# Multi-query attention of a fused decoder: score and probability banks apart, the value product in halves, the bias on GpSimd

## What is computed

```python
qkv = einsum('bsd,ed->bse', layernorm(x), Wqkv_w) + Wqkv_b
q = qkv[..., :256].reshape(B, S, 16, 16).transpose(0, 2, 1, 3)
k = qkv[..., 256:272]
v = qkv[..., 272:]
scores = einsum('bhqd,bkd->bhqk', q, k) * 16 ** -0.5
scores = where(causal, scores, finfo.min)
attn = softmax(scores, axis=-1)
ctx = einsum('bhqk,bkd->bqhd', attn, v).reshape(B, S, 256)
x = x + einsum('bsd,ed->bse', ctx, out_w) + out_b
```

## Time and profile before

| | |
|---|---|
| median of 3 runs | 3217.69 us (3211.05 to 3225.68) |
| the profiled execution | 3207.37 us, span 3205.5 us |
| PE busy over the span | 2644.7 us (83%) |
| DVE busy | 2030.2 us (63%) |
| ACT busy | 1581.7 us (49%) |
| POOL busy | 1372.7 us (43%) |

### The profile page before, as it was taken

The page is one execution under the profiler, slowest core; times in us unless marked ns, Lnnn a source line. Parts: engine busy times, 40 slices in busy tenths (PEclk is TensorE's granted clock), DMA queues, the critical chain, the costliest instruction groups (busy, mean ns, idle before and its releaser), DMA issues. The chain is left out here.

```text
span 3205.5 us, 85997 instructions
## 1 busy us (share of the span) xinstructions
PE 2644.7 (83%) x33006; PEld 1936.5 (60%) x33006; DVE 2030.2 (63%) x3706; ACT 1581.7 (49%) x2950; POOL 1372.7 (43%) x1490
## 2 busy tenths in 40 slices
PE   3888888888858888867677779999999999997565
PEld 2677777777732222224466667888788888886333
DVE  6888888888858888848577743434343434334776
ACT  3555555555527777731334313443434444443566
POOL 4888888888822333224222212222222212221665
PEclk9999999999969999979799989999999999999667
DMA  3000000000013333300100020000000000000000
GB/s 120 2 0 0 0 0 0 0 0 0 0 49 89 89 90 90 92 13 0 31 24 25 26 69 6 7 6 7 6 7 6 7 6 7 5 33 1 13 16 23
DMA packets 94784, 77.50 MB, mean 24 GB/s; under 512 B 17520, under 2 KB 88560, under 8 KB 93424
## 3 DMA queue, kind: packets, MB, share of 16 engines
q1 hardware_dynamic: 94576, 74.35, 7.6%
HBM read 55.97 MB, written 17.04 MB: 23 GB/s over the span
## 5 line engine op out<-in xcount | busy, mean ns | idle before, releaser
L1394 DVE TENSOR_REDUCE x_mx<-x_ps 128x2 f16<-128x512 f32 x512 | 330.8, 682 | 47.0 <-PE x_ps L1458 44.5
L1363 ACT ACTIVATE x_e<-x_ps 128x512 f32<-128x512 f32 x512 | 291.9, 596 | 46.2 <-PE x_ps L1462 30.2
L361 POOL TENSOR_TENSOR x1s<-x1s,x1mx 128x1024 f32<-128x1024 f32 x32 | 60.9, 1902 | 542.3 <-DVE x1mx L357 542.3
L1722 ACT ACTIVATE x_q<-x_ps,x_q_bias,x_q_scale 128x128 f32<-128x128 f32 x512 | 186.1, 467 | 162.0 <-PE x_ps L105 161.9
L1458 PE MATMUL x_ps<-x_k,x_q 32*128 32x256 f16 x1024 | 194.7, 281 | 82.4 <-ACT x_e L1363 53.1
L431 ACT CAST x1oh<-x_ps 128x1024 f16<-128x1024 f32 x64 | 64.7, 1012 | 328.9 <-PE x_ps L423 328.9
L103 PE MATMUL a_ps<-ln_xha,a_wq 128*128 128x128 f16 x1024 | 181.0, 222 | 51.3 <-ACT a0v L678 43.8
L1458 PEld LDWEIGHTS x_ps<-x_k,x_q 32*128 32x128 f16 x1024 | 58.7, 92 | 261.6 <-DVE x_mx L1394 126.2
L627 POOL TENSOR_TENSOR a_w<-a_qsw,a_tab 128x512 f32<-128x512 f32 x128 | 176.8, 1381 | 58.1 <-ACT a_qsw L688 56.7
L1462 PE MATMUL x_ps<-x_q,x_k 32*128 32x256 f16 x1024 | 196.5, 283 | 1.7 <-ACT x_e L1363 1.4
L280 DVE TENSOR_TENSOR ln_xlx<-x_ps,ln_xhx 128x256 f16<-128x256 f32 x32 | 13.6, 424 | 289.0 <-ACT x_xt L1714 289.0
(11 more groups left out here) (365 smaller groups left out, 9120.4 us busy)
## 6 DMA issues: line engine op xcount, KB each, us to landing
x_q<-x_q_rows SPq DMA_DIRECT2D x32, 256.0 KB, 2.8
x_k<-x_k_rows SPq DMA_DIRECT2D x32, 256.0 KB, 3.1
a_stage<-in_x_w SPq DMA_DIRECT2D x32, 256.0 KB, 2.6
x_vt<-in_ctx_v SPq DMA_DIRECT2D x32, 144.0 KB, 2.3
stage<-in_x_wt SPq DMA_DIRECT2D x4, 1028.0 KB, 6.4
x_all<-in_x SPq DMA_DIRECT2D x8, 512.0 KB, 9.9
x_cf<-in_ctx SPq DMA_DIRECT2D x32, 128.0 KB, 2.1
x_q_rows<-x_xhl SPq DMA_DIRECT2D x32, 128.0 KB, 1.7
```

What stands on the lines that cost most here:

```text
L1363: act.activation(e[:, u % ES].rearrange("p c n -> p (c n)"), s2_ps(u), ACT.Exp, scale=XT ** -0.5).then_inc(e_ready, 1)
L1394: dve.reduce_max(mx[:, p % 2, c:c + 2], s1_ps(u), AX).then_inc(mx_ready, 1)
L1722: last = act.activation(q[:, i, :], ps[:, bank(4 + g), h * P:(h + 1) * P], ACT.Identity, scale=q_scale[:, i:i + 1], bias=q_bias[:, i:i + 1])
```

## The change

It touches only `attention_mqa`:

- The PSUM banks are dealt anew. Scores keep banks 4 and 5; the transposed probabilities get banks 2 and 3; the output projection `y` goes beside the layer-norm transpose in bank 0, and the transposed result `ot_ps` beside the value product in bank 7. scores(t) now waits for the subtraction of the maximum of t-1 (`s_ready`) in place of the copy of its transposed probabilities.
- PE's step becomes scores(t), first half of products(t-1), a wait for ln.low(t+1), output(t-2), front(t+1), second half of products(t-1), transpose(t), ln.transpose(t+2), transpose_o(t-1). transpose(t) is in its own step, no longer in the next one.
- The output bias is added to x by POOL (`add_bias`, L2140) after the normalisation has read x; DVE's `add` is one instruction.
- DVE's step becomes low(t-2), ln.low(t+1), stats(t+2), maximum(t), add(t-2), values(t+1), weights_low(t-1), normalise(t+2), divide(t-1), denominator(t). ACT's `high` is one tile later, ahead of ln.high.

```diff
-        ot_ps = ps[:, 2, 0:2 * P].rearrange("p (b n) -> p b n", b=2)
-        y = ps[:, 3, 0:DM]
+        ot_ps = ps[:, 7, P:3 * P].rearrange("p (b n) -> p b n", b=2)
+        y = ps[:, 0, DM:2 * DM]
         sc = ps[:, 4:6, :].rearrange("p a (h s) -> p (a h) s", s=SEQ)
-        ptp = ps[:, 4:6, :].rearrange("p a (h s) -> p (a h) s", s=P)
+        ptp = ps[:, 2:4, :].rearrange("p a (h s) -> p (a h) s", s=P)
...
+            def add_bias(t):
+                pool.wait_ge(ln.xn_ready, t + 1)
+                x = m.x_all[:, at(t), :]
+                pool.tensor_tensor(x, x, o_bias[:, :], ALU.add).then_inc(biased, 1)
...
                 if has_next:
                     diagonal_keys(t + 1, 1 - p)
+                    add_bias(t + 1)
...
                 dve.wait_ge(y_ready, t + 1)
+                dve.wait_ge(biased, t + 1)
                 x = m.x_all[:, at(t), :]
-                dve.scalar_tensor_tensor(x, y, 1.0 / WS, x, ALU.mult, ALU.add).then_inc(y_added, 1)
-                dve.wait_ge(y_added, t + 1)
-                dve.tensor_tensor(x, x, o_bias[:, :], ALU.add).then_inc(x_done, 1)
+                dve.scalar_tensor_tensor(x, y, 1.0 / WS, x, ALU.mult, ALU.add).then_inc(x_done, 1)
...
             def scores(t, p):
                 pe.wait_ge(kd_ready, t + 1)
                 if started(t, 1):
-                    pe.wait_ge(pt_ready, t)
+                    pe.wait_ge(s_ready, t)
...
-            def products(t, p):
-                pe.wait_ge(pt_ready, t + 1)
-                pe.wait_ge(v_ready, t + 1)
-                wait_used(pe, o_ready, t, 1)
-                for k in range(AG):
+            def products(t, p, r):
+                if r == 0:
+                    pe.wait_ge(pt_ready, t + 1)
+                    pe.wait_ge(v_ready, t + 1)
+                    wait_used(pe, o_ready, t, 1)
+                    wait_used(pe, ol_ready, t, 1)
+                for k in range(r * AG // 2, (r + 1) * AG // 2):
...
             def step(t, p, has_next):
+                scores(t, p)
                 if started(t, 1):
-                    transpose(t - 1)
-                if has_next:
-                    ln.transpose(pe, t + 1, 1 - p)
+                    products(t - 1, 1 - p, 0)
+                if has_next:
+                    pe.wait_ge(ln.xl_ready, t + 2)
                 if started(t, 2):
                     output(t - 2)
                 if has_next:
                     front(t + 1, 1 - p)
-                scores(t, p)
                 if started(t, 1):
-                    products(t - 1, 1 - p)
+                    products(t - 1, 1 - p, 1)
+                transpose(t)
+                if further(t):
+                    wait_used(pe, x_done, t, 2)
+                    ln.transpose(pe, t + 2, p)
+                if started(t, 1):
                     transpose_o(t - 1)
```

More of the change, by code:

```diff
@@ L2098, in attention_mqa @@
             sem(n) for n in ("ptr_ready", "pt_ready", "pv_ready", "o_ready", "ot_ready", "oh_ready", "ol_ready"))
-        y_ready, y_added, x_done = sem("y_ready"), sem("y_added"), sem("x_done")
+        y_ready, biased, x_done = sem("y_ready"), sem("biased"), sem("x_done")
         proj = ps[:, 1, :]
-        ot_ps = ps[:, 2, 0:2 * P].rearrange("p (b n) -> p b n", b=2)
-        y = ps[:, 3, 0:DM]
+        ot_ps = ps[:, 7, P:3 * P].rearrange("p (b n) -> p b n", b=2)
+        y = ps[:, 0, DM:2 * DM]
         sc = ps[:, 4:6, :].rearrange("p a (h s) -> p (a h) s", s=SEQ)
-        ptp = ps[:, 4:6, :].rearrange("p a (h s) -> p (a h) s", s=P)
+        ptp = ps[:, 2:4, :].rearrange("p a (h s) -> p (a h) s", s=P)
         o_ps = ps[:, 6:8, 0:P]
@@ L2144, in head @@
                 diagonal_keys(0, 0)
+                add_bias(0)
             def step(t, p, has_next):
@@ L2187, in step @@
                     copy_transposed(t - 1)
+                if started(t, 2):
+                    high(t - 2)
                 if has_next:
@@ L2191, in step @@
                 exponential(t)
-                if started(t, 1):
-                    high(t - 1)
                 act.wait_ge(piece_in[p], (t - p) * 8 + 16)
@@ L2197, in _ @@
             copy_transposed(TILES - 1)
+            high(TILES - 2)
             high(TILES - 1)
@@ L2262, in step @@
                 ch.tile(t)
+                if started(t, 2):
+                    low(t - 2)
                 if has_next:
                     ln.low(dve, t + 1, 1 - p)
+                if further(t):
+                    ln.stats(dve, ch, t + 2, p)
+                maximum(t)
                 if started(t, 2):
                     add(t - 2)
-                if further(t):
-                    ln.stats(dve, ch, t + 2, p)
+                if has_next:
+                    values(t + 1, 1 - p)
+                if started(t, 1):
+                    weights_low(t - 1, 1 - p)
                 if further(t):
                     ln.normalise(dve, t + 2, p)
-                maximum(t)
                 if started(t, 1):
                     divide(t - 1)
-                if has_next:
-                    values(t + 1, 1 - p)
                 denominator(t)
[L2277 to L2280, removed]
             over_tiles(dve, head, step)
             weights_low(TILES - 1, 1)
+            low(TILES - 2)
+            add(TILES - 2)
             divide(TILES - 1)
             low(TILES - 1)
-            add(TILES - 2)
             add(TILES - 1)
@@ L2332, in products @@
                         last = pe.matmul(o_ps[:, b, k * AD:(k + 1) * AD], pt[rows, k, :], v[rows, p, :], start=True, stop=True)
-                last.then_inc(pv_ready, 1)
+                if r:
+                    last.then_inc(pv_ready, 1)
             def transpose_o(t):
@@ L2351, in head @@
                 front(0, 0)
+                ln.transpose(pe, 1, 1)
                 pe.wait_ge(mask_set, 1)
             def step(t, p, has_next):
+                scores(t, p)
                 if started(t, 1):
-                    transpose(t - 1)
+                    products(t - 1, 1 - p, 0)
                 if has_next:
-                    ln.transpose(pe, t + 1, 1 - p)
+                    pe.wait_ge(ln.xl_ready, t + 2)
                 if started(t, 2):
@@ L2362, in step @@
                     front(t + 1, 1 - p)
-                scores(t, p)
                 if started(t, 1):
-                    products(t - 1, 1 - p)
+                    products(t - 1, 1 - p, 1)
+                transpose(t)
+                if further(t):
+                    wait_used(pe, x_done, t, 2)
+                    ln.transpose(pe, t + 2, p)
+                if started(t, 1):
                     transpose_o(t - 1)
             over_tiles(pe, head, step)
-            transpose(TILES - 1)
             output(TILES - 2)
-            products(TILES - 1, 1)
+            products(TILES - 1, 1, 0)
+            products(TILES - 1, 1, 1)
             transpose_o(TILES - 1)
```

2 lines of the change are left out of this document (1 added, 1 removed).

## The result

| | before | changed |
|---|---|---|
| median | 3217.08 us | 3273.03 us (3268.26 to 3276.71) |
| ratio, 95% interval | 1 | 1.0171 [1.0144, 1.0198] |
| profiled execution, its span | 3207.37, 3205.5 us | 3273.39, 3271.5 us |
| start of the first key spread `a_kd` | 1541.15 | 1546.76 |
| from there to the start of the last one ("stage") | 318.3 us | 372.6 us |

The forecast was 3213 us, its range ended at 3234; the time is outside it, on the side that had a chance of 0.09. Of the 66.0 us by which the spans differ, 54.3 lie in the stage. (Before's median is now that of four executions, 3217.08 in place of 3217.69.)

A forecast was written before the change was run, and what follows sets the result against it. No engine was full; a ring of waits bound the MQA stage at 10.24 us per tile. A new ring of 10.26 gave +0.6 us over 28 tiles, head and tail -5, so -4 in all: 3213 us, range 3189 to 3234.

The forecast's parts named there:

- The lock-out: MQA loop: DVE with two SBUF inputs waits while POOL runs; `weights_low` behind `a_kd` (1.90 us), expected 1.46 us per tile lost.
- The other order at the lock: Rival: `weights_low` gets in before `a_kd`, or normalisation passes the bias addition; 9.70 or 9.67 us per tile, 3198 us; chance 0.20.
- the same 0.13: POOL's bias addition after its wait: 0.72 us alone, shortened by 0.13 to 0.59.
- the 0.41 called an addition: Earlier trace: normalisation `L262` took 0.80 us beside POOL, in place of 0.41 for an addition of the same width.
- The ring: Dependency chain from scores(t) to scores(t+1) in the MQA loop; 10.26 us with the lock-out, against 10.24 before.
- without lock-out: Rival: `weights_low` is not blocked by POOL; ring of 8.78 us per tile, 3172 us; chance 0.10.
- the steps into other tile shapes: Steps between PE's sections, about 0.1 us each at two places per tile; bounds nothing to twice that.
- PE's rows at 1.00: Ring's sum used PE durations at granted clock 1.00, 2.4 GHz.
- the lower clock: Rival: longer PE waits bring half clock, doubling some 5.3 us of ring; six tiles give 3241 us; chance 0.08.
- 200 us at 1.00 with 2.5 us of waits per tile: Argument against the lower clock: the kernel before held full clock over 200 us despite such waits.
- Both signs: For the lower clock: PE waits of about 0.9 and 1.4 us, longer than 1.03; clock 0.57 from 1864 to 1868.
- Head and tail: MQA stage's ends: -3 us at the head (0 to -6), -2 at the tail (0 to -4), together -5.

The follow-up runs named there:

- e1: Changed kernel with `weights_low` moved to the end of VectorE's step, behind the denominator; 3220.12 us, ratio 0.9996.
- e3: Changed kernel with both PE waits filled by identity transposes, 8 before the exponential's and 10 before the normalised tile's; 3191.95 us, ratio 0.9911.
- e7: Changed kernel with only PE's first wait, for the exponential, filled by 8 identity transposes; 3183.34 us, ratio 0.9901.
- e6: The order of e2 with 8 identity transposes before PE's wait for the exponential; 3136.54 us, ratio 0.9769.
- e10: The order of e2 with 88 idle two-column matmuls at the head of PE's MQA stream, none in the loop; 3176.56 us, ratio 0.9886.
- e5: Kernel before the change with 88 idle two-column matmuls at the head of PE's MQA stream; 3196.44 us, ratio 0.9941.
- e9: Changed kernel with 88 idle two-column matmuls at the head of PE's MQA stream, nothing in the loop; 3242.05 us, ratio 1.0105.
- e2: Changed kernel with `weights_low` last and the normalisation right behind `add`, ahead of `values`; 3204.35 us, ratio 0.9955.
- e11: e10 with three identity transposes per tile before PE's wait for the exponential; 3143.99 us, ratio 0.9786.
- e12: e1 with 8 identity transposes before PE's wait for the exponential; 3153.16 us, ratio 0.9800.
- e8: Changed kernel with only PE's second wait, for the normalised tile, filled by 10 identity transposes; 3204.07 us, ratio 0.9946.
- e4: Changed kernel with the output bias added by DVE again and `add_bias` out; 3264.98 us, ratio 1.0139.

## Why the prediction was wrong

**The lock-out was right, in its mechanism and in its size.** Forecast: `a_kd` first by 0.1 us; measured 1699.25 against L2249's 1699.47, 0.22. Forecast: weights end 0.53 behind it, bias 0.59 behind that, normalisation 0.15 later; measured 0.54, 0.60 and 0.14. The Trainium skill, page "SBUF — State Buffer", section "Who interferes with whom", says that whichever of the two issues second is blocked for the whole instruction of the other; the trace agrees (L2249 stands from 1699.47 to the end of `a_kd` at 1701.15 and takes 2.19 us in the mean, 0.68 in e1 where POOL is idle). The other order at the lock, which had 0.20, did not come: `a_kd` is first in the tile shown, and the least of the 25 times of L2249 from 1600 to 1900 us is 2.14. Two slips of the working are too small to matter: the bias addition was shortened by "the same 0.13" where `L535` had saved 0.15, and the 0.41 called an addition in the earlier trace rows is the division.

**The ring was right at full clock.** Forecast 10.26, measured 10.35 and 10.33 in e3 and e7; without lock-out forecast 8.78, measured 8.64 in e6. The lock-out costs 10.33 less 8.64, 1.69 us per tile, where the text had 1.48. With 8.64 below the 8.78, the steps into other tile shapes leave no sign of more than the 0.10 taken.

**The step that failed is the clock.** The sum was made with PE's rows at 1.00, and the lower clock was a rival with 0.08, on the ground of "200 us at 1.00 with 2.5 us of waits per tile". That ground does not bear: it adds up waits of different places. The kernel before has 0.28, 1.03, 0.32 and 0.58 us of waits per tile, PE busy 79%, and stays at 1.00; e10 has one wait of 0.92 in a tile of 8.64, so PE busy for 89% of it, and falls. What the runs show in place of "PE's rows at 1.00" is a clock of 0.76 to 0.80. The rival was mis-sized as well, in both factors: it doubled 5.3 us of PE's ring in four to six tiles, while the half clock covers only the work right behind the waits, 1.9 us per tile (12.29 less 10.35), but in every tile. Over all 31 periods, the short first ones included, the mean is 12.02 against 10.25 in e3, which is the 54.9 us between the two stages.

Both signs stood in the text: waits "longer than the 1.03 of now", and the tail of the kernel before at 0.57 "after waits much like the steady ones" (there the wait ahead of the output is 0.73 us in place of 0.58, the others are the same). They weighed more than the 200 quiet microseconds, and 0.08 was too little for them.

**Head and tail.** The five microseconds forecast can't be told in the time: the start of the first key spread alone varies between 1540 and 1557 us among the runs without padding, whose stages ahead of MQA are the same code. Inside the stage the head can be told: the first three periods sum to 31.6 us before, 29.6 in the changed kernel, and 28.1 in e3 at full clock, so 2.0 to 3.4 us less, against the 3 forecast (0 to 6). Padded against padded, the rest is 1328.2 us in e5 and 1325.0 in e9; the -2 for the tail is of that size, but the key spread also stands elsewhere in the step. The DMAs of the weight pieces, `high` a tile later and the wait for `x_done` cost nothing: none is among PE's waits.

**What stays open.** Which wait lets the clock fall, and when. Not the sum of the waits (before and e10), not the longest one alone (e7 holds 1.00 with 1.3 us behind the transposes, e10 falls with 0.92 ahead of them), and not the tile by itself (e2 and e10 run eight and six short tiles and then none again, with the same waits). What the runs do show: the wait of 0.9 us or more for `a_e`, which follows the small matmuls of the value product, is in each kernel that fell; halving it (e11) or filling it (e6, e7, e12) held the clock each time, and filling only the other one (e8) most of the time. The small matmuls alone can't be it: before, they stand ahead of the longest wait too, and the clock held. No run varied them.

## What to carry to other kernels

When a change makes the waits of TensorE fewer but longer, price its work at both clocks and give the lower one a real chance, even where the old loop stood at 1.00 with more idle time; then try a few useless transposes ahead of the longest steady wait, since three of them (a wait of 0.92 us cut to 0.44) were worth 33 us here. Before a DVE instruction with two SBUF inputs, or a normalisation, is moved, lay it beside POOL's queue: here three places further down took 58 us off the stage. And compare the stage that was edited, from event to event, since the length of the code ahead of a later loop can move the total by 20 us.

## What was not expected of the hardware

- **The clock can fall in a loop whose TensorE is busy for 89% of the time and whose longest wait is 0.92 us**, after six or eight such tiles in which it held, and then stay down (e2, e10); 0.44 us at the same place is harmless (e11).
- **A later loop on PE stood still 13 times for 0.9 to 1.9 us** for nothing that the profile names, 16 to 21 us in all, in the kernels with the original length of code ahead of it (before, changed, e1, e2, e4), and not at all in those with some 40 or more instructions added ahead of it (e3, e5 to e12). The Trainium skill, page "Runtime: NRT & Kernel Launch", section "Instruction fetch mechanics", has instructions fetched in blocks while the engine runs and calls the cost of crossing one "mostly hidden", but adds that a taken branch to a place outside the blocks at hand must wait for a fetch. The 13 still-stands in 13 jumps back would fit the second, though they come 11 or 15 matmuls behind the jump; no run showed the fetch itself.
